# Two tile sizes for the experts, the last norm in their block, and a residual addition moved from POOL to DVE

## What is computed

```
x = layernorm(x + attn(x))            # linear attention: softmax(q) over 16 channels, softmax(k) over tokens
x = layernorm(x + cross(ctx, x))      # 8 heads, 77 keys per batch, keys and values straight from ctx, masked
x = layernorm(x + ffn(x))             # router softmax, top 4 of 8 experts, weights renormalised
ffn: h = gelu(x @ up[e]);  y = h @ down[e];  output = sum over the 4 chosen experts of weight * y
```

## Time and profile before

| | |
|---|---|
| median of 3 runs | 1358.94 us (1358.13 to 1359.33) |
| the profiled execution | 1359.07 us |
| its span in the profile | 1357.2 us |
| PE busy (matmuls) | 1149.5 us, 85% |
| DVE, POOL, ACT busy | 760.5, 690.2, 483.1 us |
| mean granted TensorE clock | 0.905 of full |

### The profile page before, as it was taken

How to read it: one execution, slowest core, us unless ns; L and a number is a source line. 1 busy time by engine, 2 the same in 40 slices (tenths; PEclk the granted TensorE clock), 3 DMA queues, 4 the chain that set the end, 5 groups by cost and what they waited for, 6 DMA issues and landing times. The chain is left out here.

```text
span 1357.2 us, 27232 instructions
## 1 busy us (share of the span) xinstructions
PE 1149.5 (85%) x8690; PEld 953.7 (70%) x8690; DVE 760.5 (56%) x1826; ACT 483.1 (36%) x909; POOL 690.2 (51%) x783
## 2 busy tenths in 40 slices
PE   6689778888777770499999999999999999999950
PEld 3456556566565550388888888888888888888840
DVE  2458778769867664244554455445544455445516
ACT  2235454444543520233333333333333333333312
POOL 3024277557837766344554455545554555455424
PEclk9889898788877765699999999999999999999985
DMA  4112222322313210245544444445544444444427
GB/s 129 54 55 93 75 81 77 102 67 63 110 56 98 70 31 12 63 69 81 77 77 80 78 77 79 81 73 81 78 82 77 78 78 80 77 80 77 75 25 247
DMA packets 172144, 106.64 MB, mean 79 GB/s; under 512 B 109820, under 2 KB 165168, under 8 KB 171760
## 3 DMA queue, kind: packets, MB, share of 16 engines
q1 hardware_dynamic: 140656, 66.59, 19.7%
q0 software_dynamic: 31360, 38.30, 17.6%
HBM read 51.35 MB, written 34.87 MB: 64 GB/s over the span
## 5 line engine op out<-in xcount | busy, mean ns | idle before, releaser
L1246 PE MATMUL psu<-xT,w_up 128*128 128x256 f16 x3408 | 386.3, 274 | 36.4 <-DMA xT<-xg 36.4
L1214 POOL DMA_INDIRECT token_sums<-y,rec x142 | 235.8, 1661 | 335.9 <-ACT y L1291 311.3
L1246 PEld LDWEIGHTS psu<-xT,w_up 128*128 x3408 | 334.8, 98 | 76.4 <-issue 36.5
L1261 PE MATMUL psy<-w_down,hh 128*128 x2272 | 375.8, 273 | 0.0
L1261 PE MATMUL psy<-w_down,hl 128*128 x1136 | 309.6, 273 | 0.0
L1283 ACT ACTIVATE h<-psu,up_scale 128x512 f32<-128x512 f32 x284 | 195.1, 687 | 173.9 <-PE psu L1246 159.9
L1261 PEld LDWEIGHTS psy<-w_down,hh 128*128 128x128 f16 x2272 | 222.3, 98 | 25.7
L1317 DVE SCALAR_TENSOR_TENSOR hl<-h,h_scale,hh 128x512 f16<-128x512 f32 x284 | 213.4, 751 | 10.1
L1305 DVE TENSOR_SCALAR gate<-rec,y_scale 128x2 f32<-128x2 f32 x71 | 16.2, 229 | 310.3 <-ACT y L1291 294.3
L1315 DVE TENSOR_SCALAR hh<-h,h_scale 128x512 f16<-128x512 f32 x284 | 139.1, 490 | 76.8 <-ACT h L1283 71.8
L1291 ACT ACTIVATE y<-psy,gate 128x256 f32<-128x256 f32 x142 | 59.5, 469 | 329.1 <-PE psy L1261 329.1
(11 more groups left out here) (204 smaller groups left out, 1273.3 us busy)
## 6 DMA issues: line engine op xcount, KB each, us to landing
w_down<-in_L_ffn_up_w_dram SPq DMA_DIRECT2D x8, 1024.0 KB, 5.4
w_down<-in_L_ffn_down_w_dram SPq DMA_DIRECT2D x7, 1024.0 KB, 6.1
XA<-in_x_dram SPq DMA_DIRECT2D x32, 128.0 KB, 2.4
XRES<-in_x_dram SPq DMA_DIRECT2D x32, 128.0 KB
token_sums<-X SPq DMA_DIRECT2D x32, 128.0 KB, 3.8
token_rows<-XR SPq DMA_DIRECT2D x32, 128.0 KB
sums<-token_sums SPq DMA_DIRECT2D x8, 512.0 KB, 7.5
out_dram<-sums SPq DMA_DIRECT2D x8, 512.0 KB, 2.9
```

The costliest lines, as they stand in the source:

```text
L1214: pool.indirect_dma_start(acc, bass.IndirectOffsetOnAxis(ap=rec[:, t % RING, j, 0:1], axis=0), y[:, t % 2, j, :], None, compute_op=ALU.add ...
L1246: ins = pe.matmul(psu[use % UBANKS][:, i * SLOTS:(i + 1) * SLOTS], w[:, ws, c, m:m + P], xT[:, t % 2, xs * CC + c, :], start=(n == 0), sto ...
L1261: ins = pe.matmul(ytile(t)[:, j, :], (hh, hl)[hs][:, t % 2, c, j * P:(j + 1) * P], w[:, ws, c, :], start=(n == 0), stop=(n == 3 * HC - 1))
```

## The change

Tiles come in two sizes. Of each expert's list, full tiles of 256 are cut first (at most `FULL` = 63 over all experts), and what remains is cut into tiles of 128; `ETILES` becomes 63 + 9 = 72, with 135 blocks of 128 tokens where there were 142. All 63 full tiles come first in the loop. `parts(t)` is 2 for a full tile and 1 for a half one, `size(t)` 256 or 128, `chunks(t)` how many hidden chunks share a bank of 512 columns (2 or 4). Every loop and semaphore count follows these. `tile_tables` makes both kinds. PE loads the expert's number once per tile. The last norm's code moves into the experts block behind each engine's loop; SP waits for the landings instead of POOL, the view of memory gives partition p the tokens 32p to 32p+31 in place of every 128th, and DVE normalises 1 tile of a group and ACT 3. The second residual is added by DVE ahead of the routing.

```diff
-ETILES = (TOPK * B * N + EXP * (SLOTS - 1)) // SLOTS
+BLOCKS = (TOPK * B * N + EXP * (P - 1)) // P
+FULL = (BLOCKS - EXP) // SB
+ETILES = FULL + BLOCKS - SB * FULL
...
-            def second_residual(g):
-                pool.wait_ge(x1_ready, g + 1)
-                pool.wait_ge(sm_free, SM["pv", g] + 1)
-                pool.tensor_tensor(X2[:, g % 3, :], X2[:, g % 3, :], X1[:, g % 3, :], ALU.add).then_inc(r2_ready, 1)
...
-                if c3 is not None:
-                    second_residual(c3)
...
+                if c3 is not None:
+                    dve.wait_ge(sm_free, SM["pv", c3] + 1)
+                    dve.wait_ge(x1_ready, c3 + 1)
+                    dve.tensor_tensor(X2[:, c3 % 3, :], X2[:, c3 % 3, :], X1[:, c3 % 3, :], ALU.add).then_inc(r2_ready, 1)
                 for half in range(HALVES):
...
-                done(dve.tensor_reduce(tiles[:, :], cmpt[:, :, :], AX_X, ALU.add))
+                done(dve.tensor_reduce(blocks[:, :], cmpt[:, :, :], AX_X, ALU.add))
+                done(dve.tensor_reduce(tiles[:, :], cmpt[:, :, 1:PER:2], AX_X, ALU.add))
                 done(dve.tensor_tensor_scan(endt[:, :], ones[:, 0:EXP], tiles[:, :], 0.0, ALU.mult, ALU.add))
...
+                done(dve.tensor_scalar(endt[:, :], endt[:, :], float(FULL), None, ALU.min))
+                done(dve.tensor_scalar(start[:, :], start[:, :], float(FULL), None, ALU.min))
+                done(dve.tensor_tensor(tiles[:, :], endt[:, :], start[:, :], ALU.subtract))
...
+        G = 4
+        GROUPS = NT // G
+        BY_DVE = 1
...
+        sums_in = acc[0:B * N, :].rearrange("(p t) c -> p t c", p=P)
+        normed_out = out.rearrange("b n c -> (b n) c").rearrange("(p t) c -> p t c", p=P)
...
+        def parts(t):
+            return SB if t < FULL else 1
+        def size(t):
+            return P * parts(t)
...
+        def chunks(t):
+            return 512 // size(t)
...
+            for t in (ETILES - 2, ETILES - 1):
+                sp.wait_ge(y_added[t % 2], moved(t))
+            for g in range(GROUPS):
+                sp.dma_start(s[:, g * G:(g + 1) * G, :], sums_in[:, g * G:(g + 1) * G, :]).then_inc(sums_loaded[g], 16)
...
-            for t in (ETILES - 2, ETILES - 1):
-                pool.wait_ge(y_added[t % 2], added(t))
...
-                for g in range(NG):
-                    use = NG * t + g
+                for g, use in enumerate(groups(t)):
                     if use >= UBANKS:
                         pe.wait_ge(gelu_ready, use - UBANKS + 1)
-                    for i in range(GRP):
-                        m = (GRP * g + i) * P
+                    for i in range(chunks(t)):
+                        m = (chunks(t) * g + i) * P
                         n = 0
                         for c in range(CC):
                             for ws, xs in ((0, 0), (0, 1), (1, 0)):
-                                ins = pe.matmul(psu[use % UBANKS][:, i * SLOTS:(i + 1) * SLOTS], w[:, ws, c, m:m + P], xT[:, t % 2, xs * CC + c, :],
+                                ins = pe.matmul(psu[use % UBANKS][:, i * size(t):(i + 1) * size(t)], w[:, ws, c, m:m + P], xT[:, t % 2, xs * CC + c, 0:size(t)],
                                                 start=(n == 0), stop=(n == 3 * CC - 1))
...
+            before = expert_of(0)
+            up_products(0, before)
             for t in range(1, ETILES):
-                up_products(t)
-                down_products(t - 1)
-            down_products(ETILES - 1)
+                now = expert_of(t)
+                up_products(t, now)
+                down_products(t - 1, before)
+                before = now
+            down_products(ETILES - 1, before)
...
+                for i in range(g * G + BY_DVE, (g + 1) * G):
+                    act.activation(s[:, i, :], s[:, i, :], ACT.Identity, scale=frstd[:, i:i + 1], bias=fshift[:, i:i + 1]).then_inc(normed_s, 1)
```

More of the change, by code:

```diff
@@ L49 @@
 ROOT_BIAS = 2.0 ** 64
-PER = N * B // SLOTS
+PER = N * B // P
 HTARGET = 2.0 ** 10
@@ L195, in layer_kernel @@
         attention(nc, k, rows, acc, slots, x, ctx, mask, Wq, bq, Wk, bk, Wv, bv, Wo, bo, ln_g, ln_b, xb, router, up, down)
-        experts(nc, k, rows, acc, slots)
-        last_norm(nc, k, acc, out)
+        experts(nc, k, rows, acc, slots, out)
 def attention(nc, k, rows, acc, slots, x, ctx, mask, Wq, bq, Wk, bk, Wv, bv, Wo, bo, ln_g, ln_b, xb, router, up, down):
@@ new lines, in tile_tables @@
+                for at, base, size in ((slice(0, FULL), first, SLOTS), (slice(FULL, ETILES), expert_slot, P)):
+                    n_at = at.stop - at.start
+                    done(dve.tensor_tensor(parts[:, at, :], hot[:, at, :], base[:, :].unsqueeze(1).to_broadcast([P, n_at, EXP]), ALU.mult))
+                    done(dve.tensor_reduce(slot_sum[:, at], parts[:, at, :], AX_X, ALU.add))
+                    done(dve.scalar_tensor_tensor(out=k["tile_slot"][:, at], in0=iof[:, 0:n_at], scalar=float(size), in1=slot_sum[:, at], op0=ALU.mult, op1=ALU.add))
@@ L1133, in _, with experts @@
             pe.matmul(small_into(("cnt",))[:, 0:EXP], ones[:, :], counted[:, :, 0], start=True, stop=True).then_inc(sm_ready, 1)
-def experts(nc, k, rows, acc, slots):
+def experts(nc, k, rows, acc, slots, out):
     st = ExitStack()
@@ L1167, in experts @@
         gate_ready, table_loaded = sem("gate_ready"), sem("warm_ready")
+        G = 4
+        GROUPS = NT // G
+        BY_DVE = 1
+        s = sb("sums", [P, NT, C])
+        fstat = sb("fstat", [P, 2, 6])
+        fmv = sb("fmv", [P, NT, 2])
+        fvar = sb("fvar", [P, NT])
+        frstd = sb("frstd", [P, NT])
+        fprod = sb("fprod", [P, NT])
+        fshift = sb("fshift", [P, NT])
+        sums_loaded = [sem(f"sums_loaded{g}") for g in range(GROUPS)]
+        fstats_ready, fmv_ready, fvar_ready, frstd_ready, fprod_ready, fshift_ready = (
+            sem("fstats_ready"), sem("fmv_ready"), sem("fvar_ready"), sem("frstd_ready"), sem("fprod_ready"), sem("fshift_ready"))
+        normed_v, normed_s, stored = sem("normed_by_vector"), sem("normed_by_scalar"), sem("stored")
+        sums_in = acc[0:B * N, :].rearrange("(p t) c -> p t c", p=P)
+        normed_out = out.rearrange("b n c -> (b n) c").rearrange("(p t) c -> p t c", p=P)
         block = st.enter_context(nc.Block())
@@ L1171, in ytile, with parts_to, moved, groups_to @@
             return psy[t % 2][:, 0:SB * C].rearrange("p (j c) -> p j c", c=C)
-        def added(t):
-            return 16 * SB * (t // 2 + 1)
+        def parts(t):
+            return SB if t < FULL else 1
+        def size(t):
+            return P * parts(t)
+        def parts_to(t):
+            return sum(parts(u) for u in range(t + 1))
+        def moved(t):
+            return 16 * sum(parts(u) for u in range(t % 2, t + 1, 2))
+        def chunks(t):
+            return 512 // size(t)
+        def groups_to(t):
+            return sum(HC // chunks(u) for u in range(t + 1))
+        def groups(t):
+            return range(groups_to(t) - HC // chunks(t), groups_to(t))
         @block.sync
@@ L1201, in gather @@
                 if t >= 2:
-                    pool.wait_ge(xt_loaded[t % 2], added(t - 2))
+                    pool.wait_ge(xt_loaded[t % 2], moved(t - 2))
                 pool.wait_ge(rec_loaded[t % RING], 16 * (t // RING + 1))
-                for j in range(SB):
+                for j in range(parts(t)):
                     pool.indirect_dma_start(xg[:, t % 2, j, :], None, rows,
@@ L1277, in gelus @@
             def gelus(t):
-                for g in range(NG):
-                    use = NG * t + g
+                for use in groups(t):
                     act.wait_ge(up_ready, use + 1)
@@ L1364, in norm_group @@
             def norm_group(g):
-                dve.wait_ge(rstd_ready, g + 1)
-                for i in range(g * G, g * G + G // 2):
-                    dve.tensor_scalar(s[:, i, :], s[:, i, :], mv[:, i, 0:1], rstd[:, i:i + 1], ALU.subtract, ALU.mult).then_inc(normed_v, 1)
+                dve.wait_ge(frstd_ready, g + 1)
+                for i in range(g * G, g * G + BY_DVE):
+                    dve.tensor_scalar(s[:, i, :], s[:, i, :], fmv[:, i, 0:1], frstd[:, i:i + 1], ALU.subtract, ALU.mult).then_inc(normed_v, 1)
```

154 lines of the change are left out of this document (61 added, 93 removed).

## The result

The changed kernel takes 1327.57 us (median of 4 runs, 1325.90 to 1328.67) against 1358.54 us (1358.05 to 1359.33) for the kernel before on the same chip: 0.977, 95% interval 0.9754 to 0.9787. That is 31.0 us less, where 37.9 were forecast, and inside the range. The profiled execution took 1327.34 us, its span 1325.6.

What follows compares the result with a forecast made beforehand. It took PE's array to bound the experts, and neither PE nor DVE alone the attention stage. Terms -22.8 - 1.8 - 5.8 + 0.4 - 2.1 - 6.0 = -38.1 took 1359.07 to 1321.0 us, range 1311 to 1334.

Steps and rivals of the forecast that it cites:

- Part 1: Experts, tile sizes: eight full periods go, nine half tiles of 7.1 us come; minus 22.8 us.
- with half the columns the sequencer becomes the slower one: Half tiles' up phase: PE's sequencer needs 86 ns per pair of load and matmul, 7.1 us per half tile.
- plus 1 for the last down phase: End of the half tiles: last down phase set by the array, waiting a little for its last input; plus 1 us.
- Parts 2 and 3: Experts' end, minus 1.8; last norm in the same block: drain minus 5.8, its end plus 0.4, norm minus 2.1 us.
- Part 4: Attention stage: second residual added by DVE instead of POOL; minus 6 us, bounds plus 4 and minus 13.
- the price: Attention stage: each DVE addition costs 0.45 us, from L734's 0.416 and a gap of about 0.03.
- the path: Attention stage: DVE's 17.1 us of waits in 18 steps for POOL's addition go; 9.0 won after DVE's own cost.
- The 16 last scatters: Sign at the attention stage's end: last block of 16 scatters starts near 518 to 520 us instead of 526.4.
- A: Half tiles: sequencer is no limit, 128 columns cost half; up to minus 36, 1308 us, or 1314 with minus 30; chance 0.10.
- B: Half tiles: a pair of 128 columns takes 98 to 109 ns on the array; gain 13, total 1331 us; chance 0.10.
- C: Half tiles: array gaps drop the clock to its low level; plus 15 us, total 1359 or 1365; chance 0.08.
- D: Attention stage: DVE's addition makes DVE late, plus 4 instead of minus 6; total 1331 us; chance 0.10.

Runs made afterwards that it cites:

- e5_fixed_expert: Changed kernel with PE taking expert 0's weights at fixed addresses in the nine half tiles, so no register operation per weight address: 1315.74 us, 0.9687.
- e2_dve_add: Kernel before with only the second residual addition moved from POOL to DVE: 1358.99 us, 0.9999.
- e9_dve_longer: Changed kernel with two unused DVE reductions of 256 columns behind each new addition: 1339.19 us, 0.9855.
- e10_tiny_add: Changed kernel with DVE's addition of the second residual covering 1 column instead of 256: 1327.40 us, 0.9771.
- e7_bias_first: Changed kernel with POOL's other addition (first residual plus bias, L522) ahead of a step's scatters instead of between them: 1322.07 us, 0.9742.

## Why the prediction was right, and where it was wrong

**Part 1, right to 0.3 us, and for the reason given.** 87 ns per pair for 86, period 7.05 for 7.1, first two up phases 2.86 and 2.96 for 3.1. The step "with half the columns the sequencer becomes the slower one" is shown by `e5_fixed_expert`. The plus 1 for the last down phase was too much: the last two down phases follow each other without a gap over 0.12 us. So a part of the agreement to 0.3 us is luck.

The page that was weighed there, the Trainium skill, "TensorE: Matmul & The Clock Gate", section Back-to-back issue gap, gives about 81 ns per pair of load and matmul in a stream for N=128 and about 56 ns for an isolated matmul. The measured stream of 48 pairs has 55.7 ns, so the measurement decides for the smaller figure here.

**Parts 2 and 3, right to 0.6 us.** Together -9.3 forecast, -9.5 measured. The end of the experts gave 7.2 of 7.6, the stretch behind it 2.3 for 1.7. The drain at the end was taken at the old block's 5.44 us; it took 4.62 and hides. The norm loop's groups are 2.92 apart for 2.86, and the view costs nothing, as assumed.

**Part 4, wrong: nothing for -6 (+0.9 by the landmark, -0.1 by `e2_dve_add`), in the bounds, and the whole miss.** Two steps failed. The first is the price: "L734, 0.416, with a gap of about 0.03". In the kernel before, L734 never runs beside one of POOL's additions of 128x256, only beside scatters and operations of a few columns. The new addition does meet one: in the kernel before, POOL's residual addition stood ahead of L520 in the queue and waited there for DVE's X2, holding L520 back; with it gone L520 (L522 now) moved up to where DVE adds. 15 of 32 additions take 0.86 to 1.05 us (all 32 take 7.9 us more than the forecast has), the 16 splits 2.6 more than before, and POOL's other addition 16.9. The forecast looked at what POOL's queue loses behind the moved step, and not at what moves up into its place; it weighed the rule that the two engines delay each other, but for POOL's `rstd` operations alone. The cost was there to see, as POOL's 2.77 us beside L701; I took it for one that the change removes, and it moved to L522 (8 of 32 over 1.5 us, before 1).

The second is the path: 17.1 us of DVE's waits on POOL were counted as won. They are gone in the profile, and the stage is no shorter. `e9_dve_longer` passes half to two thirds of an added length on; `e10_tiny_add` nothing of one taken away. That the stage is bound by DVE, by PE and its clock, and by POOL in turn fits this, but it is argued, not shown. The 16 last scatters, forecast at 518 to 520, start at 526.27; in `e7_bias_first`, with the overlap gone, at 517.3 in an execution 4.2 us faster than that kernel's median. So about the forecast's gain was to be had, in another order of the queue.

**Rivals.** A had the array's price right (55.7 ns) and its condition wrong: the sequencer is the limit. Without that limit, in `e5_fixed_expert`, the experts are 35.8 us shorter than before, A's minus 36. That its 1314 is near that kernel's 1315.74 is luck: it has minus 30 in place of 36, and 6 for part 4 that didn't come. B is out by the same run. C is out: the clock stayed at 1.00 through the half tiles, though by starts the array was without work for about a quarter of the time in seven of them. D named the right place; its +4 was nothing that can be told from zero.

**Two slips in the sums.** B's "8.2 x 9 = 71" is 74, so its part 1 gives 10, not 13, and its total 1334, not 1331. And "two thirds of that, minus 30" is a little over half of the way from 22.8 to 36. Neither touches the forecast of 1321.0; with two thirds, about 31.6, the range would begin 1 to 2 us lower.

## What to carry to other kernels

Before an operation is moved between two engines that delay each other, as DVE and POOL do here, write down what will run beside it at its new time, the neighbours that move up included; a duration from a row without such a neighbour is a lower bound. Where weights or operands are addressed through a register, price a small matmul by the sequencer's operations per pair as well as by its columns, and take the longer, and put small tiles behind large ones, whose down phase gives the sequencer time to run ahead. A wait removed is time only if nothing else is as late: one run with the operation longer and one with it shorter tell how much of it counts. And where executions of the same code differ by the granted clock, look at the clock before a few microseconds are put down to an edit.

## What the runs showed of the hardware

- A matmul of 128 moving columns with 128x128 weights in f16 and its own weight load goes at 55.7 ns per pair on the array at full clock, and at 87 ns where two register operations stand to three pairs. The recorded lengths, 219 to 227 ns and 96 to 98 ns, hardly differ between the two.
- Two-input operations of DVE and POOL on SBUF delay each other: 0.88 for 0.41 on DVE with 0.95 for 0.73 on POOL; POOL's 2.83 and the split's 2.77 for 2.35. A DVE addition of one column is delayed as much (0.61 for 0.15) as one of 256. POOL's scatters don't delay DVE's addition (0.43 beside one), but one beside the split takes up to 3.0 us for 0.96. The Trainium skill, "SBUF — State Buffer", section SBUF: two separate sides, says that of a DVE operation with two SBUF inputs and a POOL operation that reads SBUF the one that starts first holds the shared ports for its whole instruction and the other is blocked. The kernel before agrees: POOL's addition starts 0.16 us behind the split, the split keeps its 2.35, and POOL ends 0.58 us behind it. In the change POOL's L522 ends 0.58 behind the split too, but the split, though first by 0.5 us, takes 2.77; and in the row of 347.70 DVE is recorded as first by 0.5 us and is the one that is long. Those two the rule doesn't explain by the recorded starts.
- POOL's drain at the end of a block with scatters and gathers took 5.44 to 5.76 us in kernels with 71 tiles of 256 (three of them), and 4.29 to 4.62 in those with half tiles (eleven); 1.37 behind the attention block. Why isn't tested.
- The granted clock stayed at 1.00 over seven half tiles of 7.05 us in which the array had some 1.8 us without work each (an estimate: 7.05 less the 5.3 us that such a tile takes in `e5_fixed_expert`), in pieces so short that no two matmuls start more than 0.25 us apart.
- The granted clock of one and the same attention block differs from execution to execution: step 8 had it at 0.87 and 1.00 in two kernels with the changed block, and at 1.00 and 0.83 in two with the block before, and took 2.3 and 1.8 us more at the lower one.
